# The q, k and v products in three F32R passes of split operands, with a reordered read pipeline

## The reference, cut to what matters

```python
def rat_read(res, W, gamma, beta, num_outputs):
    x = res.reshape(b, l, H, C)                      # H = 512, C = 4
    y = jnp.einsum('blhc,hoc->bloh', x, W)           # three outputs: for q, k, v
    yn = (y - y.mean(-1)) * rsqrt(y.var(-1) + EPS)
    return (yn * gamma + beta).reshape(b, l, num_outputs * H)
q, k, v = jnp.split(qkv_in, 3, axis=-1)
q = einsum('bli,oi->blo', q, qkv_w[0])               # 512 x 512, the same for k and v
q, k = rope(q, pos), rope(k, pos)
```

## Time and profile before

| | value |
|---|---|
| median of 3 runs | 1674.73 us |
| the profiled execution's own time | 1670.99 us |
| its span | 1669.2 us |
| PE busy | 1545.9 us, 93% |
| DVE busy | 1142.0 us, 68% |
| ACT busy | 906.8 us, 54% |
| POOL busy | 337.0 us, 20% |
| mean granted TensorE clock | 0.968 of full |
| project stage, first instruction to last v product | 0 to 270.6 us |

### The profile page before, as it was taken

The page is one execution under the profiler, slowest core; times in us unless marked ns, Lnnn a source line. Parts: engine busy times, 40 slices in busy tenths (PEclk is TensorE's granted clock), DMA queues, the critical chain, the costliest instruction groups (busy, mean ns, idle before and its releaser), DMA issues.

```text
span 1669.2 us, 24979 instructions
## 1 busy us (share of the span) xinstructions
PE 1545.9 (93%) x9430; PEld 1159.3 (69%) x9430; DVE 1142.0 (68%) x1790; ACT 906.8 (54%) x1672; POOL 337.0 (20%) x327
## 2 busy tenths in 40 slices
PE   7999999999999985799999999799999999999976
PEld 6565555666666653678898777697778788875554
DVE  7877754888888866753473685874786864636776
ACT  5334235888888864555543656553557724552443
POOL 1434435555434500020002000012000002000001
PEclk8999999999999996799999999999999999999997
DMA  9658567999987735367677765567665656656632
GB/s 359 218 195 309 179 170 232 275 292 281 269 222 206 214 129 204 114 237 238 209 225 236 246 227 202 173 234 237 236 243 200 230 189 223 223 186 210 222 147 101
DMA packets 129624, 364.81 MB, mean 219 GB/s; under 512 B 15968, under 2 KB 45280, under 8 KB 114144
## 3 DMA queue, kind: packets, MB, share of 16 engines
q1 hardware_dynamic: 129216, 363.08, 67.1%
q10 hardware_dynamic: 288, 0.13, 0.0%
HBM read 277.04 MB, written 86.11 MB: 218 GB/s over the span
## 4 chain that ended last, share of the span: by engine, by line
PE 76%; DVE 13%; ACT 6%; issue 3%; DMA 2%; POOL 0%; SPq 0%; DVEq 0%; ACTq 0%
PE ps L1654 21%; PE ps L1666 8%; PE ps L561 7%; PE ps L1054 5%; PE ps L1041 4%; PE ps L1077 4%; PE ps L1566 4%; PE ps L1679 4%; PE ps L1597 3%; ACT a_p L1156 3%; PE ps L1551 3%; PE ps L1612 3%; PE ps L520 3%; PE ps L1624 2%; PE ps L533 1%
## 5 line engine op out<-in xcount | busy, mean ns | idle before, releaser
L1654 PE MATMUL ps<-m_y_split,m_win 128*128 128x512 f32 x1536 | 376.0, 398 | 2.9 <-issue 2.9
L1654 PEld LDWEIGHTS ps<-m_y_split,m_win 128*128 128x128 f32 x1536 | 285.1, 189 | 64.5 <-issue 7.5
L1098 DVE TENSOR_REDUCE a_negmax<-ps 128x1 f32<-128x640 f32 (+7 forms) x176 | 180.6, 1026 | 59.6 <-PE ps L1044 58.8
L1156 ACT ACTIVATE a_p<-ps,a_negmax 128x128 f32<-128x128 f32 (+7 forms) x256 | 188.6, 750 | 29.2 <-DVE a_negmax L1098 26.8
L1666 PE MATMUL ps<-m_wods,m_y_split 128*128 128x316 f32 x768 | 178.2, 321 | 3.0 <-DVE m_hT L1854 2.6
L1892 ACT ACTIVATE m_turned<-ps 128x512 f32<-128x512 f32 x128 | 75.1, 594 | 162.6 <-PE ps L1551 148.6
L1054 PE MATMUL ps<-ident,a_p 128*128 128x128 f32 x1152 | 157.6, 275 | 1.4 <-DVE a_pT L1111 1.2
L1041 PE MATMUL ps<-a_k,a_q 128*128 128x512 f32 (+3 forms) x384 | 123.9, 402 | 16.2 <-ACT a_p L1156 14.3
L1666 PEld LDWEIGHTS ps<-m_wods,m_y_split 128*128 128x128 f32 x768 | 127.7, 191 | 7.9 <-issue 3.9
L1054 PEld LDWEIGHTS ps<-ident,a_p 128*128 128x128 f32 x1152 | 123.7, 142 | 3.4 <-DVE a_pT L1111 1.9
L2039 POOL TENSOR_TENSOR m_scale<-m_scale,mhalf 128x2 f32<-128x2 f32 x16 | 12.0, 747 | 538.3 <-DVE m_scale L1790 538.3
(11 more groups left out here) (219 smaller groups left out, 2925.9 us busy)
## 6 DMA issues: line engine op xcount, KB each, us to landing
m_win<-mlp_in_split SPq DMA_DIRECT2D x128, 512.0 KB, 4.3
m_wods<-mlp_out_split SPq DMA_DIRECT2D x96, 316.0 KB, 3.3
m_wod<-in_wod1T SPq DMA_DIRECT2D x64, 316.0 KB, 2.9
p_xT<-in_xT SPq DMA_DIRECT2D x16, 1024.0 KB, 9.1
p_x<-in_x SPq DMA_DIRECT2D x16, 1024.0 KB, 10.5
a_q<-qk_split SPq DMA_DIRECT2D x64, 256.0 KB, 7.1
a_k<-qk_split SPq DMA_DIRECT2D x128, 128.0 KB, 7.2
mlp_in_split<-a_w_two SPq DMA_DIRECT2D x32, 512.0 KB, 5.8
```

The costliest lines, as they stand in the source:

```text
L1098: V.tensor_reduce(negmax[:, n % 4, 0:len(units[n][3])], by_head(n, score_banks(n)), AX_X, ALU.max, negate=True).then_inc(max_ready, 1)
L1156: m = S.activation(dst[:, j, :], src[:, j, :], ACT.Exp, bias=negmax[:, n % 4, j:j + 1], accum_out=rsum[:, si % 2, q * 4 + hh:q * 4 + hh + 1])
L1654: m = nc.tensor.matmul(bank_of("m", blk, step), win[s][:, wl, ic, :], y[k], start=(ic == 0 and p3 == 0), stop=(ic == HCH - 1 and p3 == 2))
```

## The change

Three things are changed, all in the project stage.

1. Every q, k and v product is made of three F32R matmuls: upper half of y by upper half of w, upper by lower, lower by upper. The weights are split once: ACT rounds (`weights_upper`, 12 activations), DVE subtracts for q and v, POOL for k. The activations are split in every turn: ACT writes the upper half (`yh`, F32R) and the whole value is written too (`yT`, in the place of the lower half), by DVE for chunks 0, 1, 4, 5 and by a second activation for the other eight; then the lower half is a subtraction, by DVE for chunks 0 and 1 and by POOL for the other ten.
2. The order. The turn is in three parts: w = 0 (q) and w = 1 (k) stand between two blocks, w = 2 (v) stands before n4. PE's reads follow steps 0, 3, 5, 7; read_a of the next tile is at steps 0, 3, 5, 8; read_b at 0, 3, 5, 7; the last y on ACT at step 10.
3. The buffers. There are five y slots for six, three rope slots (written in place, `hi` and `lo` in the slot) for two, one table of cos and sin for two, one `p_v` for two. The first heads are loaded in the last block, at steps 0 and 3.

```diff
-            return 6 * blk + k // 4
+            return 6 * blk + (0, 1, 3)[k // HCH]          # turn1_before
-            return 6 * blk + 3 + n // 4
+            return 6 * blk + (2, 4)[n // 4]               # qk_before
+        RAW_BY_DVE, LO_BY_DVE = (0, 1, 4, 5), (0, 1)
+        def halves_are_free(e, blk, w):
+            if w == 1:
+                e.wait_ge(v_mm, 4 * blk)
+            else:
+                e.wait_ge(qk_mm, 8 * blk + 2 * w)
-        READ_AT = {3 * t: (t, 0) for t in range(TB)} | {3 * t + 1: (t, 1) for t in range(TB)}
+        READ_AT = {0: 0, 3: 1, 5: 2, 7: 3}
+        MOMENTS_AT = {0: 1, 3: 2, 5: 3, 8: 4}
+        Y_AT = {0: 0, 3: 1, 5: 2, 10: 3}
+        def moments_at(blk, step):
+            tiles = [0] if (blk, step) == (0, 0) else []
+            tiles += [MOMENTS_AT[step]] if step in MOMENTS_AT else []
+            return [i for i in ((blk + 1) * TB + t for t in tiles) if i < NT]
...
 (PE, qkv)
+                    if n == 4:
+                        turn(blk, 2)
                     pe.wait_ge(emptied[b], qk_before(blk, n))
                     for ic in range(HCH):
                         k = w * HCH + ic
-                        m = nc.tensor.matmul(ps[:, b, :], wq[:, k, col:col + P], yT[:, k, :],
-                                             start=(ic == 0), stop=(ic == HCH - 1))
+                        upper_is_there(blk, k)
+                        for j, ww in enumerate((whi, wlo)):
+                            nc.tensor.matmul(ps[:, b, :], ww[:, k, col:col + P], halves_of(blk, k)[0],
+                                             start=(ic == 0 and j == 0), stop=False)
+                    for ic in range(HCH):
+                        k = w * HCH + ic
+                        lower_is_there(blk, k)
+                        m = nc.tensor.matmul(ps[:, b, :], whi[:, k, col:col + P], halves_of(blk, k)[1],
+                                             start=False, stop=(ic == HCH - 1))
...
 (DVE)
+                raw(0)
+                raw(1)
+                lower(0)
+                lower(1)
+                raw(4)
+                raw(5)
...
-                dve.wait_ge(lo_ready, 2 * u - 2)
+                dve.wait_ge(split_stored[s], rope_stored_before(u, s))
...
+            for k in range(HCH):
+                dve.wait_ge(whi_ready, k + 1)
+                m = V.scalar_tensor_tensor(out=wlo[:, k, :], in0=wraw[:, k, :], scalar=QSCALE,
+                                           in1=whi[:, k, :].bitcast(F32), op0=ALU.mult, op1=ALU.subtract)
             turn(0)
+            for k in range(2 * HCH, 3 * HCH):
+                dve.wait_ge(whi_ready, k + 1)
+                V.tensor_tensor(wlo[:, k, :], wraw[:, k, :], whi[:, k, :].bitcast(F32),
+                                ALU.subtract).then_inc(wvlo_ready, 1)
                 for step in range(12):
                     if step < 8 and step % 2:
                         rope(blk, step // 2)
+                    for i in moments_at(blk, step):
+                        read_a(i)
+                    for i in read_at(blk, step, READ_AT):
+                        read_b(i)
...
 (ACT)
+            def turn(blk, w):
+                for k in range(HCH * w, HCH * w + HCH):
+                    act.wait_ge(turn1_mm, 12 * blk + k + 1)
+                    halves_are_free(act, blk, w)
+                    S.activation(yhi_, ps[:, b, :], ACT.Identity, bias=..., scale=...).then_inc(y1hi_ready, 1)
+                    if k not in RAW_BY_DVE:
+                        S.activation(whole, ps[:, b, :], ACT.Identity, bias=..., scale=...).then_inc(emptied[b], 1)
...
-            turn(0)
+            weights_upper(0)
+            for w in range(2):
+                turn(0, w)
+            weights_upper(1)
+            weights_upper(2)
             for blk in range(NBLK):
                 for step in range(12):
+                    if step == 3:
+                        turn(blk, 2)
                     if step < 8 and step % 2:
                         round_rope(blk, step // 2)
                     if step >= 8:
                         values(blk, step - 8)
+                    for i in read_at(blk, step, Y_AT):
+                        read_b(i)
...
 (POOL)
+            lower(0, range(2, 2 * HCH))
+            for k in range(HCH, 2 * HCH):
+                G.tensor_tensor(wlo[:, k, :], wraw[:, k, :], whi[:, k, :].bitcast(F32),
+                                ALU.subtract).then_inc(wklo_ready, 1)
                 for step in range(12):
                     if step < 8 and step % 2:
                         rope(blk, step // 2)
+                    for i in moments_at(blk, step):
+                        read_a(i)
+                    for i in read_at(blk, step, READ_AT):
+                        read_b(i)
+                    if step == 3:
+                        lower(blk, range(2 * HCH, 3 * HCH))
+                if blk + 1 < NBLK:
+                    lower(blk + 1, range(2, 2 * HCH))
...
 (SP)
                     if step < 8 and step % 2:
                         store_qk(blk, step // 2)
+                    if blk == NBLK - 1 and step in (0, 3):
+                        load_first_heads(step)
+                    for i in read_at(blk, step, READ_AT):
+                        if i + 2 < NT:
+                            load(i + 2)
```

More of the change, by code:

```diff
@@ L278, in program @@
         reads_end = place[0]
-        wq = sb("p_wqkv", [P, 3 * HCH, H])
+        whi = sb("p_wqkv_hi", [P, 3 * HCH, H], F32R)
+        wraw_place = place[0]
+        wraw = sb("p_wqkv", [P, 3 * HCH, H])
+        place[0] = wraw_place
+        wlo = sb("p_wqkv_lo", [P, 3 * HCH, H], F32R)
         read1 = sb("p_read1", [P, DCH, RD1, HPC])
@@ L522, in read @@
                 m.then_inc(read1_mm, 1)
-            def turn(blk):
+            def turn(blk, w):
                 pe.wait_ge(ident_loaded, 16)
-                if blk == 0:
+                if blk == 0 and w == 0:
                     pe.wait_ge(z_ready, TB)
@@ L578, in project_pe @@
                 read(i)
-            turn(0)
+            for w in range(2):
+                turn(0, w)
             for blk in range(NBLK):
                 for step, _ in enumerate(qkv(blk)):
-                    if blk + 1 < NBLK and step in READ_AT and READ_AT[step][1] == 0 and (blk, step) != (0, 0):
-                        read((blk + 1) * TB + READ_AT[step][0])
+                    for i in read_at(blk, step, READ_AT):
+                        if i > TB:
+                            read(i)
                 if blk + 1 < NBLK:
-                    turn(blk + 1)
+                    for w in range(2):
+                        turn(blk + 1, w)
         BY_ACT = (1, 2, 3)
@@ L737, in project_dve @@
                         rope(blk, step // 2)
-                    if blk + 1 < NBLK and step in READ_AT:
-                        t, part = READ_AT[step]
-                        (read_b if part else read_a)((blk + 1) * TB + t)
+                    for i in moments_at(blk, step):
+                        read_a(i)
+                    for i in read_at(blk, step, READ_AT):
+                        read_b(i)
                 if blk + 1 < NBLK:
@@ L749, in project_act @@
             S.preload_act_table_set(ACT_SET)
-            spare = p_v[0][:, :, :].rearrange("p a b -> p (a b)")
+            spare = p_v[:, :, :].rearrange("p a b -> p (a b)")
             def total(i):
@@ L776, in read_b, with weights_upper, turn @@
                     m.then_inc(y1_ready, 1)
-            def turn(blk):
+            def weights_upper(w):
+                for k in range(HCH * w, HCH * w + HCH):
+                    act.wait_ge(wkv_loaded if w else wq_loaded, 16)
+                    S.activation(whi[:, k, :], wraw[:, k, :], ACT.Copy,
+                                 scale=1.0 if w else QSCALE).then_inc(whi_ready, 1)
+            def turn(blk, w):
                 act.wait_ge(scale1_loaded, 32)
-                for k in range(0, RD1 * HCH, 2):
+                for k in range(HCH * w, HCH * w + HCH):
@@ L816, in project_act @@
                         values(blk, step - 8)
-                    if blk + 1 < NBLK and step in READ_AT and READ_AT[step][1]:
-                        read_b((blk + 1) * TB + READ_AT[step][0])
+                    for i in read_at(blk, step, Y_AT):
+                        read_b(i)
                 if blk + 1 < NBLK:
-                    turn(blk + 1)
+                    for w in range(2):
+                        turn(blk + 1, w)
         def project_pool():
@@ L842, in read_b, with lower @@
                 G.tensor_tensor(p_sc[:, s, 1, :], p_sc[:, s, 0, :], mhalf[:, 0:RD1], ALU.pow).then_inc(yrstd1_ready, 1)
+            def lower(blk, ks):
+                for k in ks:
+                    yhi_, ylo_, whole = halves_of(blk, k)
+                    pool.wait_ge(emptied[4 + k % 4], turn1_before(blk, k) + 1)
+                    pool.wait_ge(y1hi_ready, 12 * blk + k + 1)
```

(4 more changed lines are left out.)

189 lines of the change are left out of this document (113 added, 76 removed).

## The result

The changed kernel takes 1704.25 us (median of 4 runs, 1702.13 to 1705.84) against 1674.71 us for the kernel before (4 runs, 1674.6 to 1674.75). The ratio is 1.0176, 95% interval 1.0158 to 1.0193: slower by 29.5 us. The prediction said slower, by 14, with 1702 as its upper end. The sign was right; the time lies outside the range. The profiled execution took 1703.46 us around a span of 1701.6.

What follows compares the result with a forecast made beforehand. TensorE bounded the old block; afterwards waits ending on VectorE would make it 63.2 us. With block 0 as if begun at 54.3 and a last block of 40.7, the stage ends 14.0 later: about 1689 us, own range 1682 to 1697, overall 1656 to 1702.

Steps and rivals of the forecast that it cites:

- arrival of x: Tile t3's x, loaded behind the stores of pair 1, lands 42.5 us into a block; VectorE stands six us too early.
- TensorE's half clock: TensorE idles some 7 us before read t3 and its clock can fall: 0.7 us a block, bounds 0 and 4.
- Products: TensorE's q, k, v products: three F32R matmuls at 0.224 us replace one F32 at 0.86; a block's 48 fall from 41.3 to 32.3.
- The block up to the third tile: Steps in a block from v's turn through pair 1's lower halves and the power to issuing x of t3 at 34.0 us.
- A: Zero point of the forecast's times in a block: where ScalarE starts the first upper half of the turn.
- The landing of x: Time from issue of t3's x load at 34.0 to its arrival, taken as 8.5 us.
- The turn: End of a steady block: VectorE done at 59.8, three ys 2.1, last copy of v 0.5; next turn at 62.5.
- The start: Before block 0: weight rounding and splitting free VectorE at about 60.3, 13 us lost; block 0 as if begun at 54.3.
- The end: Last block, without reads, 40.7 against 45.2 us; stage ends at 284.6, 14.0 later, and attention carries the shift unchanged.
- Edits costed at nothing: Rope slots, one table, one p_v, y slots and heads in the last block: no cost; heads 1 to 3 us without cover.
- the clock and the landing go the wrong way: Rival for the blocks: x lands in 10.5 us, reads run at half clock, 67 us a block, 1701 us; chance 0.13.
- The first rival: x of t3 in time, no stall of its load: 56.6 us a block, stage 5.8 earlier, 1669 us; chance 0.18.

Runs made afterwards that it cites:

- one_f32: Changed kernel with each q, k and v product as one F32 matmul of upper halves, lower-half products left out: 1723.30 us, ratio 1.0283.
- x_first: Changed kernel with the load of tile t3 issued ahead of the stores of rope pair 1 on SP: 1684.95 us, ratio 1.0053.
- keep_warm2: Changed kernel with 28 unread matmuls on TensorE ahead of the last read of a block: 1701.39 us, ratio 1.0149.
- wv_late: Changed kernel with VectorE's split of the v weights moved behind the second read (read_b of tile 4): 1695.91 us, ratio 1.0123.
- x_wv: Changed kernel with both the edits of x_first and wv_late: 1675.11 us, ratio 0.9997.
- x_wv_pow: x_wv with GpSimd taking the powers of t1 and t2 ahead of the two lower halves of pair 1: 1671.50 us, ratio 0.9974.
- best1: x_wv_pow with the last read of a block moved behind v's first tile product: 1670.10 us, ratio 0.9972.

## Why the prediction was right in sign and short by half

The mechanism was the one forecast: cheaper products, and blocks that wait for a late x and a late power. What failed are two terms of the forecast's sum for a block, and the start, which has the same two in it. The arrival of x was put at 42.5 us into the block and was 45.06; and TensorE's half clock was put at a flat 0.7 us, while TensorE's own path to the end of the block, which the sum did not follow, made the turn 2.0 us later than VectorE and ScalarE would have. In order:

- **Products.** Forecast 0.224 us from one F32R matmul to the next. In the block above the last of v's 48 starts at 189.72 and the first at 178.67: 11.05 / 47 = 0.235. The row I took it from can have records missing, and I had rounded down from its 0.229. It costs half a microsecond (48 x 0.011) ahead of v's turn. one_f32 shows that the gain was real.
- **The block up to the third tile.** Forecast: v's turn at 23.9, `lo` ended at 32.4, the power at 33.6, x of t3 issued at 34.0. Measured from A = 122.81: 24.8, 33.4, 34.7, 35.65. All steps are in place, the first three about 1 us late, the issue of x 1.65. The transfer of xT ahead of x held the queue for 1.37 us and not 0.53 as in the earlier trace rows.
- **The landing of x, the first mis-sized term.** I took 8.5 us where a row gives 7.2 at least and 10.5 in the median. It was 9.4, from an issue 1.65 late: VectorE began the moments at 45.06 and not at 42.5, 2.6 us a block, of which only 0.9 are the landing itself. x_first proves the wait itself: with it gone, a block is 61.5 and not 67.8.
- **The turn, the term that was missing.** I let VectorE end the block (59.8, then y and the copy of v) and gave the clock a flat 0.7 us, between bounds of 0 and 4. In the trace VectorE is done at 63.05 and the turn comes at 67.8. The y on ScalarE (2.2) and the last copy (0.5) would give 65.8; the other 2.0 us are TensorE's. Its read, mostly at half clock, is 2.4 us longer and all of v comes behind it. keep_warm2 gives 2.1 us back in that very block. The forecast had seen the idle time ("PE is idle for some 7 us before read t3"), and did not follow TensorE to the end of the block as a second path of equal length. Together: 62.5 + 2.6 + 0.6 (the small VectorE operation at 182.92 that lasted 1.28 us beside GpSimd, above the 0.6 already in the sum) + 2.0 = 67.7, measured 67.83.
- **The start.** Forecast: VectorE free at 60.3, turn 1 at 117.5. Measured 62.39 and 122.81. Of the first 2.1 us, 1.5 are ScalarE's: this execution's first turn began at 45.74 and not 44.2 (the other kernels with the same beginning: 43.5 to 45.9). The rest, 3.2 us, is the same late x (VectorE waited 5.99 us for it in block 0) and a last read that took 5.75 us at a clock of 0.50 in its first 3.7. wv_late proves the place of the split: 6.0 us of block 0.
- **The sum.** 5.3 (start and block 0), 4.6 and 4.7 (two steady blocks), 0.5 (the last block) are 15.1 us on top of the forecast's 14.0. Attention's start moved by 29.2.
- **The end.** The last block was forecast at 40.7, and attention's first VectorE instruction came 1.3 us behind the stage before, which makes 42.0. Measured are 42.5, against 46.5 before. That the shift would go through attention unchanged held within 3.2 us (1400.5 behind the start of attention, 1397.3 before), and closer by the medians, 29.5 us apart.
- **Edits costed at nothing** (rope slots, one table, one copy of v, y slots, heads): no wait of theirs stands among the three that fill the block, and x_wv, which keeps them all, is as fast as the kernel before.

Of the rivals, the third came nearest ("the clock and the landing go the wrong way", 67 a block, 1701), and it had 0.13. Its two causes are what the trace shows, but not at its prices: x landed in 9.4 us, not 10.5, and was late for the rest by its issue; and n0 with read t0, for which it also counted a half clock, ran at full speed (read t0 in 3.71 us at 131.49). That its sum comes so near to 67.8 is in part luck. The forecast itself took the low side of both of its open prices at once, the landing (8.5, with a median of 10.5) and the clock (0.7 of 0 to 4). The first rival ("x in time", 56.6 a block) is refuted in its price: x_first has x in time, and the block is 61.5. VectorE was done at 57.4 and not at 53.9, since the stall for the power was 4.5 us where the sum had about 3, with 2.0 more for the two slow small operations behind it; and TensorE's path added 1.4 at the end.

On the shared path of VectorE and GpSimd the prediction had left one direction without a row. It is there now: GpSimd's four subtractions of k took 6.82 us where its four of y took 5.05, while VectorE's four took 6.00 and not 2.49.

```profile
51.77 5.05 POOL L971 TENSOR_TENSOR p_yT_lo<-p_yT,p_yT_hi 128x512 fp32r<-128x512 f32 x4
56.78 6.82 POOL L1000 TENSOR_TENSOR p_wqkv_lo<-p_wqkv,p_wqkv_hi 128x512 fp32r<-128x512 f32 x4
```

5.05 + 2.49 = 7.5 us of work, and it was done in the 6.8 us from 56.78 to 63.60. In that stretch the starts of the two engines alternate, 1.7 us from one pair to the next, where one instruction of each alone takes 1.25 + 0.62 = 1.87. So they took turns, with little overlap, and both directions are real. The Trainium skill, page "SBUF — State Buffer", section "SBUF: two separate sides", states an exclusive lock that is held for a whole instruction by whichever engine has it. The trace agrees but for the 0.7 us by which the stretch is shorter than the sum.

## What to carry to other kernels

When an edit takes work from the bounding engine and moves it to others, the block becomes a chain, and each queue's order sets the time: here one load behind the four stores of a rope pair, and one weight split ahead of a read, cost 29 us; with them and two smaller places mended, the same change gains 4. Follow the engine that now stands idle to the end of the block as well as the one that is busy, since its wait costs it the clock just where its path becomes the last. Between two bounds of a price, look at what happens if both open prices go the same way before the chances are given.

## What the runs showed of the hardware

- Two instructions of three columns on VectorE (L732, with one tensor input and a scalar taken from memory, and L734, with two tensor inputs) last 1.22 and 1.20 us while GpSimd is subtracting, 0.23 and 0.16 when it is not. The two behind a late power cost 2 us in a block.
- After 8.66 us of idle time TensorE's 32 matmuls of a read took 6.13 us in place of 3.71; after 3.11 us of idle time (x_first, block 1) they took 5.41; with filling ahead and 2.23 us of idle time, 3.78; with the same filling and 2.35 us, 5.41. Without filling, x_wv_pow has 5.41 us after 2.45 (block 0) and 3.78 after 2.18 (block 1). So the idle time just ahead does not alone decide it. The granted clock was 0.50 from 172 to 177 us, in the slow read, and 1.00 from 179 to 190; over the block it was 0.92, over best1's first steady block 1.00 (window 107 to 166).
- Eight stores of two rope pairs (which wait for GpSimd's lower halves) hold SP's queue for 11.46 us from the first to the last, and a load that itself waits for nothing stays behind them: 35.65 us into the block. Ahead of the stores of pair 1 (x_first, block 1) it is issued at 142.22, 27.9 into the block, and VectorE has no wait for it left.
